# Alternating the two accumulation banks in each step of the neighbour sum of a four-layer GNN kernel

## The reference, cut to what matters

```
x = layernorm(x + L0(x, adj))   # graph convolutions on the first 25 nodes
x = layernorm(x + L1(x, adj))   # attention: softmax(masked scores) @ (x W^T + b)
x = layernorm(x + L2(x, adj))   # relu(((1 + eps) x + adj @ x) @ W1 + b1) @ W2 + b2
x = layernorm(x + L3(x, adj))   # silu(rmsnorm((eps x + adj @ x) @ W1 + b1)) @ W2 + b2
```

## Time and profile before

| | |
|---|---|
| three timed runs, median | 2726.66 us |
| the profiled execution | 2724.53 us |
| its span, first to last instruction | 2722.7 us |
| mean granted TensorE clock over the span | 0.984 of full speed |
| TensorE matmuls busy | 2608.1 us, 96% |
| TensorE weight loads busy | 2229.5 us, 82% |
| VectorE / ScalarE / GpSimd busy | 75% / 57% / 47% |
| matmuls of the sum, lines L950, L951, L954 | 1536 each |

### The profile page before, as it was taken

One profiled execution on the slowest core, in us unless ns is written; L12 is line 12 of the kernel. 1 busy time (PEld: TensorE's weight loads), 2 busy tenths in 40 slices (PEclk: granted clock), 3 DMA queues, 4 the chain that ended last, 5 costly groups with the idle time before them and its releaser, 6 DMA issues.

```text
span 2722.7 us, 41123 instructions
## 1 busy us (share of the span) xinstructions
PE 2608.1 (96%) x14650; PEld 2229.5 (82%) x14650; DVE 2030.3 (75%) x4504; ACT 1557.8 (57%) x2911; POOL 1274.9 (47%) x1385
## 2 busy tenths in 40 slices
PE   6499999999999999999999999999999999999997
PEld 5478888888888888888888888888888888888886
DVE  5776877868787786868878686886878778687735
ACT  2546557564755756466575646656475675647524
POOL 2243554535455454545535454553535555354533
PEclk8699999999999999999999999999999999999998
DMA  7040402204040220403013040311304022040200
GB/s 227 20 126 1 155 1 82 74 10 146 1 147 10 77 79 1 155 1 122 34 47 109 1 155 1 95 61 30 126 1 155 1 86 71 12 144 1 78 1 16
DMA packets 205224, 181.00 MB, mean 66 GB/s; under 512 B 17367, under 2 KB 186718, under 8 KB 205022
## 3 DMA queue, kind: packets, MB, share of 16 engines
q1 hardware_dynamic: 197454, 177.04, 20.4%
q10 hardware_dynamic: 7568, 1.34, 0.4%
HBM read 161.15 MB, written 17.19 MB: 65 GB/s over the span
## 4 chain that ended last, share of the span: by engine, by line
PE 68%; DVE 16%; ACT 8%; issue 4%; POOL 1%; ACTq 0%; DVEq 0%; POOLq 0%
PE bank L950 10%; PE bank L954 9%; PE bank L951 9%; PE bank L1015 8%; PE bank L1000 6%; PE bank L1001 6%; PE bank L1005 6%; PE bank L1029 5%; PE bank L901 3%; DVE stat L1543 3%; PE bank L1033 2%; DVE x_odd L1558 2%; DVE x_even L1558 2%; DVE hid L1627 2%; ACT hid L1251 2%
## 5 line engine op out<-in xcount | busy, mean ns | idle before, releaser
L950 PE MATMUL bank<-mt_hi,x_hi 128*128 128x512 f32 x1536 | 627.5, 409 | 0.8 <-ACT x_hi L1201 0.7
L954 PE MATMUL bank<-mt_hi,x_lo 128*128 128x512 f32 x1536 | 602.2, 392 | 0.0
L951 PE MATMUL bank<-mt_lo,x_hi 128*128 128x512 f32 x1536 | 601.1, 391 | 0.0
L1375 POOL TENSOR_TENSOR rstd<-ve,neg_half 128x4 f32<-128x4 f32 x126 | 161.3, 1280 | 416.0 <-DVE ve L1551 415.6
L954 PEld LDWEIGHTS bank<-mt_hi,x_lo 128*128 128x128 f32 x1536 | 289.2, 188 | 62.9 <-POOL x_lo L1380 0.2
L950 PEld LDWEIGHTS bank<-mt_hi,x_hi 128*128 128x128 f32 x1536 | 289.3, 188 | 56.8 <-ACT scratch L1246 6.6
L951 PEld LDWEIGHTS bank<-mt_lo,x_hi 128*128 128x128 f32 x1536 | 290.2, 189 | 49.5
L1000 PE MATMUL bank<-a_hi,W_lo 128*128 128x512 f32 x768 | 316.8, 412 | 3.7 <-ACT hid L1227 2.9
L1611 DVE TENSOR_TENSOR sq_sum<-sq_sum,scratch 128x512 f32<-128x512 f32 x224 | 154.9, 691 | 216.0 <-ACT scratch L1246 216.0
L1001 PE MATMUL bank<-a_hi,W_hi 128*128 128x512 f32 x768 | 301.7, 393 | 0.0
L1029 PE MATMUL bank<-W_hi,hid_hi 128*128 128x256 f32 x1024 | 263.0, 290 | 19.8 <-ACT hid_hi L1256 19.8
(11 more groups left out here) (169 smaller groups left out, 5978.1 us busy)
## 6 DMA issues: line engine op xcount, KB each, us to landing
att<-in_adj SPq DMA_DIRECT2D x128, 512.0 KB, 8.1
adj_col<-in_adj SPq DMA_DIRECT2D x256, 256.0 KB, 3.0
out<-x_even SPq DMA_DIRECT2D x64, 128.0 KB, 2.9
out<-x_odd SPq DMA_DIRECT2D x64, 128.0 KB, 2.7
x_odd<-in_x SPq DMA_DIRECT2D x56, 128.0 KB, 4.2
x_even<-in_x SPq DMA_DIRECT2D x49, 128.0 KB, 3.8
G<-in_L_gnn_W SPq DMA_DIRECT2D x2, 2048.0 KB, 19.0
W_raw<-in_L_gnn_W SPq DMA_DIRECT2D x2, 1024.0 KB, 10.5
```

What stands on the lines that cost most here:

```text
L950: nc.tensor.matmul(dst[:], hi, mt_hi[:, k, cols], start=k == 0, stop=False)
L951: nc.tensor.matmul(dst[:], hi, mt_lo[:, k, cols], start=False, stop=False)
L954: mm = nc.tensor.matmul(dst[:], lo, mt_hi[:, k, cols], start=False, stop=done)
```

## The change

In `agg_step` the loop over the three products becomes the outer one and the loop over `d` the inner one. Each of the three products is done for both column halves before the next. The wait for `x_lo` stands before the third product. The wait for the second bank, where a step has one, stands before the first matmul of each `d`, as before, but what stands ahead of it and behind it is different. Where a step is called for one `d` alone (layer 3, half 1, k = 6 and 7) the order stays the same. All six matmuls of a step are at one line in the kernel after, L952, and the lines behind it are one lower.

```diff
-                for d in ds:
-                    if second_bank:
-
-                        pe.wait_ge(second_bank[0], second_bank[1] - 1 + d)
-                    dst = agg_pair[h][d]
-                    hi, lo = x_hi[:, k, d * P:(d + 1) * P], x_lo[:, k, d * P:(d + 1) * P]
-                    done = k == NT - 1
-                    nc.tensor.matmul(dst[:], hi, mt_hi[:, k, cols], start=k == 0, stop=False)
-                    nc.tensor.matmul(dst[:], hi, mt_lo[:, k, cols], start=False, stop=False)
-                    if d == ds[0]:
+                done = k == NT - 1
+
+                for n, (part, mt) in enumerate(((x_hi, mt_hi), (x_hi, mt_lo), (x_lo, mt_hi))):
+                    if n == 2:
                         pe.wait_ge(s_x_lo, x_count(b, layer - 1, k))
-                    mm = nc.tensor.matmul(dst[:], lo, mt_hi[:, k, cols], start=False, stop=done)
-                    if done:
-                        mm.then_inc(s_agg, 1)
+                    for d in ds:
+                        if second_bank and n == 0:
+
+                            pe.wait_ge(second_bank[0], second_bank[1] - 1 + d)
+                        mm = nc.tensor.matmul(agg_pair[h][d][:], part[:, k, d * P:(d + 1) * P], mt[:, k, cols],
+                                              start=k == 0 and n == 0, stop=done and n == 2)
+                        if done and n == 2:
+                            mm.then_inc(s_agg, 1)
                 if k < NT - 1 and layer == 1:
                     mm.then_inc(s_att_used, 1)
```

## The result

The changed kernel is slower: 2733.6 us in the median of nine runs (2729.95 to 2736.66), against 2726.66 us (2723.2 to 2727.98) of the kernel before. The ratio is 1.0027, 95% interval 1.0018 to 1.0036. The forecast was 2733.5 us, with a range from 2727 to 2739.

A forecast was written before the change was run, and what follows sets the result against it. TensorE, busy in 96% of the span, was taken to bound the kernel, its matmul spacing deciding. Bank, weights and end of a sum 0, start of a graph +6.8: 2726.66 + 6.8 = 2733.5 us, range 2727 to 2739.

The forecast's parts named there:

- the bank: Sum's matmuls: following a matmul in another bank is no shorter than in the same one; 0 ns x 4608 = 0.
- the weights: Sum's matmuls: new weights each time cost 0, since loads of 189 ns lie inside a step of 227 ns.
- the start of a graph: First step of graphs 1 to 15: two more matmuls queue behind the second bank's wait; 15 x 0.454 = +6.8 us.
- the end of a sum: First bank completes later, a_hi of d=0 may start 0.454 us later, but other matmuls cover it; 0.
- No absorption: After a graph's start: TensorE's later waits for turned and hidden tiles take back none of the +6.8 us.
- rival 2: Layer 3, half 0: the late first bank shows, 16 x 0.454 = +7.3 us on top, 2740.8 us; chance 0.09.
- The weight loads' idle time for the squaring: Loads waiting for ScalarE's squaring at graph starts: idle time grows from 6.6 us to about 13.5 us.

The follow-up runs named there:

- experiment 1: Kernel after, but the first step of graphs 1 to 15 has the old order, banks taking turns in the other two-half steps; 2727.19 us, ratio 1.0003.
- experiment 7: No network: ten runs of 96 matmuls alone, varying bank, weights, format, columns and accumulation; 0.2267 us per matmul in float32r with 512 columns.
- Experiment 2: Banks take turns only in the first step of graphs 1 to 15, all other steps as in the kernel before; 2733.3 us, ratio 1.0026.
- experiment 3: Kernel after, with both banks' waits ahead of the first matmul in the first step of graphs 1 to 15; 2739.39 us, ratio 1.0049.
- experiment 4: Kernel before, but in graphs 1 to 15 steps 0 and 1 run for bank 0 first, then bank 1; 2722.69 us, ratio 0.9985.
- experiment 5: Kernel before, with layer 3's half 1 steps k = 4 and 5 moved beside half 0's, uncovering the eviction; old order; 2743.52 us, ratio 1.0062.
- experiment 6: As experiment 5, but banks take turns in every step except the first of graphs 1 to 15; 2751.01 us, ratio 1.0086.

## Why the prediction was right

The forecast's sum was 2726.66 + 6.8 us, and its terms for the bank, the weights, the start of a graph and the end of a sum were each measured apart. That the median came out within 0.1 us of it is luck: the nine runs spread over 6.7 us, where the forecast had taken 1.1 from three runs, and the interval of the ratio allows a loss of 4.9 to 9.8 us. The distance over the graph's end is the firmer evidence.

- **The bank and the weights, 0.** Right. The earlier trace rows had it, since the old order contained both kinds of neighbour; experiments 1 and 7 show it apart. In the changed kernel a quiet stretch reads, on TensorE:

```profile
1587.76 0.61 PE L952 MATMUL bank<-mt_lo,x_hi 128*128 128x512 f32 x2
1588.21 0.62 PE L952 MATMUL bank<-mt_hi,x_lo 128*128 128x512 f32 x2
1588.67 0.62 PE L952 MATMUL bank<-mt_hi,x_hi 128*128 128x512 f32 x2
1589.12 0.61 PE L952 MATMUL bank<-mt_lo,x_hi 128*128 128x512 f32 x2
1589.58 0.62 PE L952 MATMUL bank<-mt_hi,x_lo 128*128 128x512 f32 x2
```

  Two matmuls take 0.455 us ((1589.58 - 1587.76) / 4), 0.2275 each.
- **The start of a graph, 0.454 x 15 = +6.8 us.** Right: +0.47 in the distance over the graph's end, 15 times, +7.0. Experiment 2 puts the whole loss in this step, and experiments 3 and 4 move it up and down with the matmuls that stand behind the wait and ahead of it.
- **No absorption.** Right. Behind the first step the others start late by the same amount, which answers to the earlier trace rows: VectorE's idle time before the mean square went from 1.11 to 1.56 us, ScalarE's before silu from 6.05 to 6.50:

```profile
1581.44 0.16 DVE L1619 TENSOR_SCALAR ms<-bank 128x4 f32<-128x4 f32 x1 [1.56 <-PE bank L1046]
```

```profile
1585.55 0.63 ACT L1250 ACTIVATE hid<-hid 128x512 f32<-128x512 f32 x1 [6.50 <-DVE hid L1626]
```

- **The end of a sum, 0 behind its cover.** Right. Without the cover layer 3, half 0, pays the 16 x 0.454 us that rival 2 priced (experiments 5 and 6).
- **A detail that was off.** The weight loads' idle time for the squaring was to grow from 6.6 to 13.5 us. Line L952 has 11.8 there:

```profile
L952 PEld LDWEIGHTS bank<-mt_hi,x_hi 128*128 128x128 f32 x1536 | 270.5, 189 | 51.4 <-ACT scratch L1245 11.8 <-issue 0.8
```

  That is 0.79 a graph and not 0.90. I had added the whole 0.454 us to the loads' idle time. But a load's idle time begins where the load ahead ends: before, that load (of L954) started 0.23 us ahead of its own matmul; now it is the step's first load, which comes behind the transposes and starts only 0.03 us ahead of its matmul (1576.84 and 1576.87). The gap between matmul starts is the one to price a wait by.

## What to carry to other kernels

When a loop over independent accumulators moves inside, every wait that belongs to the second accumulator moves up in the engine's list, and each instruction that gets behind it costs about one spacing if the wait really ends late; count them. The remedy is the reverse: put independent work that needs no wait ahead of it, as in experiment 4. The same reordering makes the first accumulator complete later, which is free only as long as other work stands between it and its reader. And before pricing a rule such as "neighbours should go to different banks", look in the old trace for a place where they already do.

## What the runs showed of the hardware

- Float32r matmuls follow one another at 0.2267 us for 512 columns and 0.120 us for 256 (L78), so if the rest goes with the columns, 2 x 0.120 - 0.2267 = 0.013 us of each is fixed; that is an estimate from two sizes. Bfloat16 ones of 512 columns come at 0.215 to 0.216 us.
- The spacing is the same whether the output goes to the bank of the matmul ahead or to another, whether the weights change or not, and whether the result is accumulated or started new (L80, 21.95 us for 96, with its first distances a few ns longer).
- After a wait in mid-step the first matmul is followed by the next after 0.33 to 0.34 us and not 0.23, before and after the change. A wait that is taken away gives back this too: 0.16 + 0.11 us in experiment 4. The first matmul behind the transposes is followed after 0.30 us without any wait (1569.84 to 1570.14), and after 0.31 in experiment 3, where it has waited.
